# One product for the edge rows of both batches, first weights split ahead of the roots, and a wait for stored keys moved, in the values of a second cross-attention

## The chip, the cores and the metric

The kernel runs on one core of a Trainium2 chip. The metric is the device time of one execution in microseconds. The median of three executions is 3082.03 us (3081.09, 3082.03 and 3088.36).

Engines are named as the profile names them: PE (TensorE, matmuls), PEld (its weight loads), DVE (VectorE), ACT (ScalarE), POOL (GpSimd) and SP (SyncE, here only a queue of transfers).

## The reference, cut to what matters

The program is a decoder of two layers on x of 2 batches x 512 rows x 512 features, each layer with self-attention, cross-attention and a mixture of experts. The change lies in the cross-attention of the second layer. Its context is 2 batches x 1024 positions x 512 features. Positions 0 to 256 (257 of them) are image context with weights of their own, the others text context.

```python
def _L1_xattn_ref(x, context, q_w, q_b, k_w, k_b, v_w, v_b, ki_w, ki_b, vi_w, vi_b, o_w, o_b, nq_s, nkt_s, nki_s):
    B, S, _ = x.shape                       # 2, 512; H = 16 heads of D = 128, INNER = 2048
    img_ctx = context[:, :N_IMG]            # N_IMG = 257
    txt_ctx = context[:, N_IMG:]
    q = rms_norm(x @ q_w + q_b, nq_s).reshape(B, S, H, D)
    k_txt = rms_norm(txt_ctx @ k_w + k_b, nkt_s).reshape(B, -1, H, D)
    v_txt = (txt_ctx @ v_w + v_b).reshape(B, -1, H, D)
    out_txt = sdpa(q, k_txt, v_txt)
    k_img = rms_norm(img_ctx @ ki_w + ki_b, nki_s).reshape(B, -1, H, D)
    v_img = (img_ctx @ vi_w + vi_b).reshape(B, -1, H, D)
    out_img = sdpa(q, k_img, v_img)
    out = (out_txt + out_img).reshape(B, S, INNER)
    return out @ o_w + o_b
```

## The kernel before, in words

The code writes one instruction stream per engine by hand, in blocks, with semaphores between them. A `Stage` owns buffers and semaphores. When it closes, its semaphores are cleared and all engines meet in a barrier, so a stage ends with its slowest engine, SP's queue included. Nothing is planned by a program; the order within an engine is the order of the code, and loops (`Fori`) repeat a body.

`cross_attention1` runs four stages. `project_kq1` makes keys and queries head by head (16 heads) and stores them to DRAM, and `project_v1` makes the values. `attention_core1` reads both back, and `output_cross1` projects. All fp32 operands are held as a high part (rounded to fp32r) and a low part (the rest), and `split_matmul` (lines 2032 to 2034) makes one product of three matmuls: high x high, high x low, low x high. The context lies transposed in `ctx_high` and `ctx_low`, as 128 partitions x 4 slices of features (KC) x 2048 positions, batch 0 first.

**`project_v1`.** Its output has 2048 columns, in NG = 4 groups of 512. In a group there are UT = 16 tiles of 128 context rows (2 batches x 8). A tile's product is 4 slices x 3 matmuls = 12 matmuls. The stationary operand is 128 context positions, the moving one 512 columns of weights. `UNITS` orders the tiles, numbered from 0: four image tiles (NI = 4), then the two *edge tiles* (tiles 4 and 5, position block 2 of each batch), then ten text tiles. An edge tile holds positions 256 to 383: position 256 is image, the others text. So an edge tile is computed with the text weights, and once more with the image weights into another bank (4 + b), of which only row 0 is used:

```python
for kind, bank in [(m, t % 4)] + ([(0, 4 + b)] if kb == EDGE else []):   # line 2376
```

TensorE uses banks t % 4 and waits until the row addition four tiles back is done (`rowed`). DVE adds the bias (line 2448; for an edge tile also row 0 from the other bank, line 2452), ACT rounds to the high part (line 2411), POOL subtracts for the low part (line 2475), and SP stores both parts (line 2343), with four buffers in turn, so that ACT waits for a store four tiles back.

At the head of the stage TensorE sums the squares of the keys and queries with a matrix of ones (four matmuls of 512 columns, line 2384, and eight of one column, line 2387; each appears as two in the trace). ACT takes the roots (lines 2415 and 2419), then rounds the first image and text weights (line 2398, `split_weights`), and DVE subtracts for their low parts (line 2432). The first image weights were loaded during the keys' stage (`load_image`, line 1943). DVE takes four reciprocals of the roots (line 2456) between the tiles of the first group.

**The seam.** `project_kq1` ends, on SP, with a wait until all stored keys and queries have landed (line 2132). Its POOL adds squares up to the end (line 2282). Before the last group of `project_v1`, SP issues the core stage's first loads of keys and queries (`load_kq`, lines 1932 and 1933).

## Time and profile before

| What | Value |
|---|---|
| Timed runs: median (lowest, highest) | 3082.03 us (3081.09, 3088.36) |
| The profiled execution: its own time | 3078.52 us |
| Its span in the trace | 3076.7 us |
| Mean granted clock over it | 0.943 of full |
| TensorE busy | 2767.7 us (90%) |
| Weight loads busy | 1978.0 us (64%) |
| VectorE, ScalarE, GpSimd busy | 1461.4, 1288.5, 1108.3 us |
| Stage of the values | about 1613.8 to 1832 us |

All stretches are in microseconds from the start of the span. A matmul's busy time counts from its start to its modelled end, so matmuls overlap, and the distance from start to start is what one costs in a row of them. Weight loads run beside matmuls. The granted clock is 1.00 at 2.4 GHz and 0.50 at 1.2 GHz. An idle time is put down to the instruction that ended it. Names are the program's, without numbers: `xa` is the cross-attention, `early` the buffer of the image weights, `wt` that of the text weights, `normed` the buffer in which the rows wait, `ps` the banks.

### The profile page before, as it was taken

The page shows a single profiled execution, that of the slowest core. Times are in us where ns is not written, and L with a number is a line of the kernel's source. Part 1 is how long each engine was busy: PE and PEld are TensorE (multiplying, and loading weights), DVE is VectorE, ACT ScalarE, POOL GpSimd, SP SyncE. Part 2 cuts the span into 40 slices and gives each one's busy share as a digit, 9 for nine tenths or more (in the row PEclk, how much of TensorE's full clock was granted, in tenths as well). Part 3 has the DMA queues.
Part 4 walks back from the last instruction along what each step waited for, and adds up shares of the span by engine and source line. Part 5 has one row for each costly group of instructions (what it writes and reads, how often), then busy time and mean ns, then how long its engine had stood idle before and what let it go on. Part 6 is the DMA issues. An engine that isn't in the chain of part 4 may idle for free. (4 is left out here: it accounts for less than half of the span.)

```text
span 3076.7 us, 47541 instructions
## 1 busy us (share of the span) xinstructions
PE 2767.7 (90%) x15658; PEld 1978.0 (64%) x15658; DVE 1461.4 (47%) x2628; ACT 1288.5 (42%) x2906; POOL 1108.3 (36%) x1023
## 2 busy tenths in 40 slices
PE   7987999996699598879999989999998879999997
PEld 3453443432588345568877879999997647777762
DVE  3475436775211307678874337776663441111115
ACT  2462524554111126556652228888882202222220
POOL 2352225664111205435553445555551011212116
PEclk9899999997699798999999999999999889999998
DMA  2342424310599413156666773444431119999986
GB/s 92 70 96 82 161 87 102 64 32 4 183 326 317 155 41 83 43 181 237 236 235 192 222 233 139 184 186 174 170 150 59 50 54 339 345 346 346 345 272 210
DMA packets 320543, 526.50 MB, mean 171 GB/s; under 512 B 35778, under 2 KB 169282, under 8 KB 312228
## 3 DMA queue, kind: packets, MB, share of 16 engines
q1 hardware_dynamic: 292004, 453.61, 45.2%
q0 software_dynamic: 13440, 44.05, 4.7%
q10 hardware_dynamic: 14976, 27.27, 2.4%
q8 instruction: 69, 1.13, 0.2%
q14 instruction: 54, 0.44, 0.0%
HBM read 369.52 MB, written 130.02 MB: 162 GB/s over the span
## 5 line engine op out<-in xcount | busy, mean ns | idle before, releaser
L1741 PE MATMUL ps<-moe_blocks_xgt,moe_blocks_w 128*128 128x128 f32 (+1 forms) x3072 | 362.8, 277 | 7.1 <-DMA moe_blocks_b1s<-rb_cols 4.3
L1741 PEld LDWEIGHTS ps<-moe_blocks_xgt,moe_blocks_w 128*128 128x128 f32 (+1 forms) x3072 | 350.4, 184 | 10.3 <-issue 10.1
L2670 POOL TENSOR_TENSOR normed<-normed,xa_core_rinv 128x257 f32<-128x257 f32 (+1 forms) x256 | 260.6, 1041 | 214.0 <-DVE xa_core_rinv L2594 214.0
L1812 DVE COPY moe_blocks_y<-ps 128x512 f32<-128x512 f32 x104 | 72.0, 692 | 454.3 <-PE ps L1723 454.3
L1723 PE MATMUL ps<-moe_blocks_w,moe_blocks_ht 128*128 128x512 f32 (+1 forms) x624 | 285.0, 593 | 0.0
L550 POOL TENSOR_TENSOR sa_w<-sa_w,sa_core_rinv 128x256 f32<-128x256 f32 (+3 forms) x128 | 159.4, 1254 | 236.5 <-DVE sa_core_rinv L497 236.5
L1689 POOL COPY moe_blocks_idx<-moe_index 128x1 uint32 (+1 forms) x104 | 19.2, 185 | 561.8 <-PE ps L1714 435.2
L2650 ACT ACTIVATE normed<-normed,xa_core_nmax,xa_rq 128x257 f32<-128x257 f32 (+1 forms) x256 | 206.8, 810 | 4.2
L2282 POOL TENSOR_TENSOR normed<-normed 128x512 f32<-128x512 f32 x96 | 150.5, 1568 | 116.9 <-DVE normed L2235 116.9
L1762 ACT ACTIVATE moe_blocks_xgt<-ps 128x512 f32<-128x512 f32 x104 | 62.1, 597 | 304.1 <-PE ps L1714 304.1
L787 DVE TENSOR_REDUCE xa_nmax<-ps 128x1 f32<-128x1024 f32 x128 | 149.2, 1217 | 58.6 <-PE ps L778 58.6
L1723 PEld LDWEIGHTS ps<-moe_blocks_w,moe_blocks_ht 128*128 128x128 f32 (+1 forms) x624 | 111.0, 191 | 100.4 <-issue 100.4
L2609 DVE CUSTOM_DVE_ANT_0 normed<-ps,xa_rk 128x257 f32<-128x257 f32 (+1 forms) x256 | 164.6, 681 | 15.2 <-PE ps L2034 10.6
L527 ACT ACTIVATE sa_w<-ps,sa_core_nmax 128x128 f32<-128x128 f32 (+3 forms) x256 | 132.4, 524 | 83.5 <-DVE sa_core_nmax L493 82.3
L2600 DVE TENSOR_TENSOR xa_core_pt<-ps,xa_core_pt 128x512 fp32r<-128x512 f32 x256 | 164.6, 684 | 3.6 <-ACT xa_core_pt L2640 3.5
L2640 ACT ACTIVATE xa_core_pt<-ps 128x512 fp32r<-128x512 f32 x256 | 139.1, 596 | 64.2 <-PE ps L2572 63.8
L2032 PE MATMUL ps<-xa_core_pt,xa_core_v 128*128 128x256 f32 x512 | 155.2, 303 | 0.1
L452 PE MATMUL ps<-identity,sa_w 128*128 128x128 f32 x640 | 122.9, 302 | 30.8 <-DVE normed L506 17.1
L2034 PE MATMUL ps<-xa_core_pt,xa_core_v 128*128 128x256 f32 x512 | 144.9, 283 | 0.0
L2033 PE MATMUL ps<-xa_core_pt,xa_core_v 128*128 128x256 f32 x512 | 144.6, 282 | 0.0
L1791 ACT ACTIVATE moe_blocks_ht<-ps,moe_blocks_b1s 128x128 f32<-128x128 f32 (+1 forms) x240 | 69.9, 362 | 178.1 <-PE ps L1741 178.1
L2475 POOL TENSOR_TENSOR xa_v_parts<-normed,xa_v_parts 128x512 fp32r<-128x512 f32 x64 | 89.6, 1401 | 127.2 <-ACT xa_v_parts L2411 127.2
(333 smaller groups left out, 6525.3 us busy)
## 6 DMA issues: line engine op xcount, KB each, us to landing
moe_blocks_w<-L_ffn_rw SPq DMA_DIRECT2D x80, 704.0 KB
moe_blocks_w<-L_ffn_rw SPq DMA_DIRECT2D x80, 512.0 KB
moe_blocks_w<-L_ffn_w SPq DMA_DIRECT2D x24, 1408.0 KB
k_parts<-xa_parts SPq DMA_DIRECT2D x64, 512.0 KB, 3.3
v_parts<-xa_v_parts SPq DMA_DIRECT2D x128, 256.0 KB, 2.7
xa_parts<-k_parts SPq DMA_DIRECT2D x32, 1024.0 KB
xa_core_v<-v_parts SPq DMA_DIRECT2D x32, 1024.0 KB
moe_y<-moe_blocks_y ACTq DMA_DIRECT2D x104, 256.0 KB
```

What stands on the lines that cost most here:

```text
L550: nc.gpsimd.tensor_tensor(prob[:, 2 * s:2 * s + 2, 0:n], prob[:, 2 * s:2 * s + 2, 0:n], rinv[:, s, :, 0:1].to_broadcast([P, 2, n]), ALU.mu ...
L787: nc.vector.tensor_reduce(self.nmax[:, i % 2, m:m + 1], g.ps[:, bank:bank + 2, :].rearrange("p a n -> p (a n)"), X_AXIS, ALU.max, negate=T ...
L1723: mm = nc.tensor.matmul(g.ps[:, 6 + s % 2, :], ht[0:fn, s % 2, f, :], w2s[s][0:fn, f, :], start=(f == 0), stop=(f == NF - 1))
L1741: mm = nc.tensor.matmul(g.ps[0:fn, 2 + s % 2 + 2 * half, f * P:(f + 1) * P], w1s[s][:, k, half * F + f0:half * F + f0 + fn], xgt[:, s % 2, ...
L2032: nc.tensor.matmul(out, lhs_high, rhs_high, start=start, stop=False)
L2033: nc.tensor.matmul(out, lhs_high, rhs_low, start=False, stop=False)
L2034: return nc.tensor.matmul(out, lhs_low, rhs_high, start=False, stop=stop)
L2282: nc.gpsimd.tensor_tensor(sums[:, u * 512:(u + 1) * 512], sums[:, u * 512:(u + 1) * 512], sq[:, u % 2, :], ALU.add).then_inc(summed, 1)
L2600: nc.vector.tensor_tensor(pt[:, slot, 1, 4 * half:4 * half + 4, at:at + P], g.ps[:, 4 + half, :].rearrange("p (m q) -> p m q", m=4), pt[:, ...
L2609: ins = nc.vector.tensor_tensor_reduce(prob[:, n % PR, lo:hi], s_ps(n)[:, lo:hi], rk[:, b * CTX + lo:b * CTX + hi], 1.0, -3.4e38, ALU.mult ...
L2650: ins = nc.scalar.activation(prob[:, n % PR, lo:hi], prob[:, n % PR, lo:hi], ACT.Exp, scale=rq[:, t:t + 1], bias=nmax[:, n % PR, m:m + 1], ...
L2670: ins = nc.gpsimd.tensor_tensor(prob[:, n % PR, lo:hi], prob[:, n % PR, lo:hi], rinv[:, n % PR, m:m + 1].to_broadcast([P, hi - lo]), ALU.mult)
```

## The change

Three things change.

First, the image product of the edge rows. In a group it is computed once, in bank 4, ahead of the first edge tile (t == NI). The stationary operand is taken from the flat context with a step: 128 columns, 16 elements apart, beginning at position 256 of batch 0. Column 0 is that position, and column 64 the one 1024 further, position 256 of batch 1. The other 126 columns are not used. For the last feature slice the stepped columns run past the end of the context, so both context buffers get 256 more columns, which POOL fills with zeros in the keys' stage. DVE reads row 64 instead of row 0 for batch 1.

Second, ACT rounds the first image weights ahead of the roots, and the first text weights behind them as before.

Third, SP's wait for stored keys and queries moves from the end of the keys' stage to the place in `project_v1` right ahead of `load_kq`. The six semaphores now belong to the stage around both.

```diff
--- before.py
+++ after.py
@@ -29,6 +29,7 @@
 DX = 128
 INNER = H * DX
 NIMG = 257
+EDGE_PAD = NIMG // P * P
 LN_EPS = 1e-5
 RMS_EPS = 1e-6
 TOPK_EPS = 1e-20
@@ -1933,8 +1934,8 @@
             sp.dma_start(q[:, s, :, :].bitcast(F32), q_dram[j, :, :, :]).then_inc(kq_loaded[s], 16)
 
         with Stage(nc, name + "_made") as md:
-            ctx_high = md.sbuf("ctx_high", [P, KC, B * CTX], F32R)
-            ctx_low = md.sbuf("ctx_low", [P, KC, B * CTX], F32R)
+            ctx_parts = [md.sbuf(f"ctx_{part}", [P, KC * B * CTX + EDGE_PAD], F32R) for part in ("high", "low")]
+            ctx_high, ctx_low = [t[:, 0:KC * B * CTX].rearrange("p (k n) -> p k n", k=KC) for t in ctx_parts]
             early = md.sbuf("early", [P, KC * 512])
             wi = early[:, :].rearrange("p (k n) -> p k n", k=KC)
             wi_loaded = md.sem("wi_loaded")
@@ -1943,10 +1944,13 @@
                 sp.dma_start(wi, a["L1_xattn_vi_w"][:, bass.ds(n * 512, 512)].rearrange("(k p) n -> p k n", p=P)
                              ).then_inc(wi_loaded, 16)
 
+            stored = [md.sem(f"stored{u}") for u in range(6)]
             with Stage(nc, name + "_kq") as kq:
-                project_kq1(nc, g, kq, a, ctx_high, ctx_low, k_dram, q_dram, rk, parts, early, load_image)
+                project_kq1(nc, g, kq, a, ctx_high, ctx_low, k_dram, q_dram, rk, parts, early, load_image, stored,
+                            [t[:, KC * B * CTX:].bitcast(F32) for t in ctx_parts])
             with Stage(nc, name + "_v") as vs:
-                project_v1(nc, g, vs, a, ctx_high, ctx_low, v_dram, rk, rq, minus_rq, wi, wi_loaded, load_image, load_kq)
+                project_v1(nc, g, vs, a, ctx_high, ctx_low, v_dram, rk, rq, minus_rq, wi, wi_loaded, load_image, load_kq,
+                           stored, ctx_parts)
         ot = st.sbuf("ot", [P, B * H, S])
         with Stage(nc, name + "_core") as co:
             attention_core1(nc, g, co, k, q, kq_loaded, load_kq, v_dram, rk, rq, minus_rq, ot)
...
@@ -2064,7 +2068,6 @@
     x_highs, x_lows = st.sem("x_highs"), st.sem("x_lows")
     b_loaded, made, done, lows = st.sem("b_loaded"), st.sem("made"), st.sem("done"), st.sem("lows")
     squared, summed, zeroed = st.sem("squared"), st.sem("summed"), st.sem("zeroed")
-    stored = [st.sem(f"stored{n}") for n in range(UH)]
     scaled = st.sem("scaled")
 
     def load_weights(sp, h):
@@ -2128,8 +2131,6 @@
             sp.wait_ge(w_lows, H)
             load_image(sp, 0)
             store(H - 1)
-            for u in range(UH):
-                sp.wait_ge(stored[u], 16 * H)
 
         @block.tensor
         def _(pe):
@@ -2285,6 +2286,8 @@
             pool.wait_ge(x_lows, 1)
             nc.gpsimd.memset(sums[:, :], 0.0).then_inc(zeroed, 1)
             pool.wait_ge(zeroed, 1)
+            for pad in pads:
+                nc.gpsimd.memset(pad, 0.0).then_inc(zeroed, 1)
             head(0, 0, first=True)
             head(0, 1, first=True)
             with pool.Fori(1, H // 2) as i:
@@ -2292,7 +2295,8 @@
                 head(i, 1)
 
 
-def project_v1(nc, g, st, a, ctx_high, ctx_low, v_dram, rk, rq, minus_rq, wi, wi_loaded, load_image, load_kq):
+def project_v1(nc, g, st, a, ctx_high, ctx_low, v_dram, rk, rq, minus_rq, wi, wi_loaded, load_image, load_kq,
+               kq_stored, ctx_parts):
 
 
     NKT = CTX // P
@@ -2353,6 +2357,8 @@
             load_bias(0, 1)
             with sp.Fori(0, NG - 1) as n:
                 group(n)
+            for done in kq_stored:
+                sp.wait_ge(done, 16 * H)
             for s in range(2):
                 load_kq(sp, s, s)
             group(NG - 1, last=True)
@@ -2363,6 +2369,10 @@
         def _(pe):
             def tile(ctx, m, b, kb, k):
                 return ctx[:, k, b * CTX + kb * P:b * CTX + (kb + 1) * P]
+
+            def edges(ctx, k):
+                first, apart = k * B * CTX + EDGE * P, B * CTX // P
+                return ctx[:, first:first + apart * P:apart]
 
             def group(n, first=False):
                 pe.wait_ge(w_lows, 2 * n + 1)
@@ -2373,11 +2383,13 @@
                         pe.wait_ge(rooted, t + 1)
                     else:
                         pe.wait_ge(rowed, UT * n + t - 3)
-                    for kind, bank in [(m, t % 4)] + ([(0, 4 + b)] if kb == EDGE else []):
+                    if t == NI:
                         for k in range(KC):
-                            mm = split_matmul(nc, g.ps[:, bank, :], tile(ctx_high, m, b, kb, k), tile(ctx_low, m, b, kb, k),
-                                              w_high[:, kind, k, :], w_low[:, kind, k, :], start=(k == 0),
-                                              stop=(k == KC - 1))
+                            split_matmul(nc, g.ps[:, 4, :], edges(ctx_parts[0], k), edges(ctx_parts[1], k), w_high[:, 0, k, :],
+                                         w_low[:, 0, k, :], start=(k == 0), stop=(k == KC - 1))
+                    for k in range(KC):
+                        mm = split_matmul(nc, g.ps[:, t % 4, :], tile(ctx_high, m, b, kb, k), tile(ctx_low, m, b, kb, k),
+                                          w_high[:, m, k, :], w_low[:, m, k, :], start=(k == 0), stop=(k == KC - 1))
                     mm.then_inc(made, 1)
 
             for c in range(B * CTX // 512):
@@ -2410,6 +2422,7 @@
                         act.wait_ge(stored[t % RING], (UT // RING * n + t // RING) * 32)
                     nc.scalar.activation(parts[:, t % RING, 0, :], rows[:, t % 2, :], ACT.Copy).then_inc(highs, 1)
 
+            split_weights(0, 0)
             for c in range(B * CTX // 512):
                 act.wait_ge(total, c + 1)
                 nc.scalar.activation(rk[:, c * 512:(c + 1) * 512], g.ps[:, c, :], ACT.Sqrt, scale=1.0 / INNER,
@@ -2418,7 +2431,6 @@
             act.wait_ge(eps_put, 1)
             nc.scalar.activation(rms_q[:, :], g.ps[:, 6, 0:NT], ACT.Sqrt, scale=float(DX) / INNER,
                                  bias=eps_q[:, 0:1]).then_inc(rooted, 1)
-            split_weights(0, 0)
             split_weights(0, 1)
             group(0, first=True)
             with act.Fori(1, NG - 1) as n:
@@ -2447,9 +2459,11 @@
                         dve.wait_ge(lows, UT * n + t - 1)
                     ins = nc.vector.tensor_tensor(rows[:, t % 2, :], g.ps[:, t % 4, :], bias[:, m, :], ALU.add)
                     if kb == EDGE:
+                        at = b * (P // B)
                         ins.then_inc(edged, 1)
                         dve.wait_ge(edged, B * n + b + 1)
-                        ins = nc.vector.tensor_tensor(rows[0:1, t % 2, :], g.ps[0:1, 4 + b, :], bias[0:1, 0, :], ALU.add)
+                        ins = nc.vector.tensor_tensor(rows[0:1, t % 2, :], g.ps[at:at + 1, 4, :], bias[at:at + 1, 0, :],
+                                                      ALU.add)
                     ins.then_inc(rowed, 1)
                     if first and t in (2, 4, 6, 8):
                         c = t // 2 - 1
```

ACT, from the end of the keys' stage into the first group of the values (`xa_rk` and `xa_v_rms_q` are the roots, `xa_v_w_high` the rounded weights), before:

```order
L2199 ACTIVATE xa_parts<-ps,xa_kq_bias 128x512
L2091 UNCONDITIONAL_BRANCH
L2394 UNCONDITIONAL_BRANCH
L2415 ACTIVATE xa_rk<-ps,rms_eps 128x512 x4
L2419 ACTIVATE xa_v_rms_q<-ps,xa_v_eps_q 128x8
L2398 ACTIVATE xa_v_w_high<-xa_made_early 128x2048
L2398 ACTIVATE xa_v_w_high<-xa_v_wt 128x2048
L2411 ACTIVATE xa_v_parts<-normed 128x512 x6
L2398 ACTIVATE xa_v_w_high<-xa_made_early 128x2048
```

and now:

```order
L2200 ACTIVATE xa_parts<-ps,xa_kq_bias 128x512
L2094 UNCONDITIONAL_BRANCH
L2406 UNCONDITIONAL_BRANCH
L2410 ACTIVATE xa_v_w_high<-xa_made_early 128x2048
L2428 ACTIVATE xa_rk<-ps,rms_eps 128x512 x4
L2432 ACTIVATE xa_v_rms_q<-ps,xa_v_eps_q 128x8
L2410 ACTIVATE xa_v_w_high<-xa_v_wt 128x2048
L2423 ACTIVATE xa_v_parts<-normed 128x512 x6
L2410 ACTIVATE xa_v_w_high<-xa_made_early 128x2048
```

The rounding of the image weights (from `xa_made_early`) has moved ahead of the five roots; the rounding of the text weights (from `xa_v_wt`) stays behind them.

SP at the seam, with what each row waits for. A semaphore is printed by the name of an earlier holder of its number, so only the count of names tells something here: the six at the branch that leaves the keys' stage are the six of the stored keys and queries. Before:

```order
L2106 DMA k_parts<-xa_parts 256x1x512 [waits sa0_proj_r_loaded] x4
L2106 DMA q_parts<-xa_parts 128x1024 [waits sa0_proj_r_loaded] x2
L2091 UNCONDITIONAL_BRANCH [waits xa0_proj_inverted,xa0_proj_shifted,xa0_proj_scaled,xa0_proj_clipped,xa0_proj_tops,xa0_proj_ctx_loaded1]
L2324 UNCONDITIONAL_BRANCH [waits barrier_Pool_Activation_PE_DVE_SP_release]
L2327 DMA xa_v_wt<-L_xattn_v_w 128x4x512
L2331 DMA xa_v_bias<-L_xattn_vi_b 128x512
```

and now, at the same place:

```order
L2109 DMA k_parts<-xa_parts 256x1x512 [waits xa0_proj_scaled] x4
L2109 DMA q_parts<-xa_parts 128x1024 [waits xa0_proj_scaled] x2
L2094 UNCONDITIONAL_BRANCH
L2328 UNCONDITIONAL_BRANCH [waits barrier_Pool_Activation_PE_DVE_SP_release]
L2331 DMA xa_v_wt<-L_xattn_v_w 128x4x512
L2335 DMA xa_v_bias<-L_xattn_vi_b 128x512
```

SP now ahead of the last group of the values:

```order
L2335 DMA xa_v_bias<-L_xattn_v_b 128x512
L2358 REGISTER_ALU
L2358 COMPARE_AND_BRANCH
L1933 DMA xa_parts<-k_parts 128x2048 [waits init_x_loaded2,init_x_loaded3,init_x_loaded1,init_loaded,init_x_loaded0,init_rstd_done]
L1934 DMA xa_parts<-q_parts 128x1024
```

The six waits have left the branch and stand at the first load of keys (line 1933 of the new file). On TensorE the program has 24 rows fewer, 12 in the group written out and 12 in the loop's body, and no row in another order. POOL has two memsets more, of 256 columns each, behind the one that clears the sums in the keys' stage.

## Rows read from the trace of the kernel before

**Rows 1.** The page: busy us, share of the span, instructions.

```profile
PE 2767.7 (90%) x15658; PEld 1978.0 (64%) x15658; DVE 1461.4 (47%) x2628; ACT 1288.5 (42%) x2906; POOL 1108.3 (36%) x1023
```

**Rows 2.** Groups, 1607.2 to 1832 us: busy, mean ns, idle before.

```profile
L2032 PE MATMUL ps<-xa_v_w_high,xa_made_ctx_high 128*128 128x512 f32 x288 | 113.4, 394 | 4.5 <-DVE xa_v_w_low L2432 4.5
...
L2475 POOL TENSOR_TENSOR xa_v_parts<-normed,xa_v_parts 128x512 fp32r<-128x512 f32 x64 | 89.6, 1401 | 127.2 <-ACT xa_v_parts L2411 127.2
...
L2448 DVE TENSOR_TENSOR normed<-ps,xa_v_bias 128x512 f32<-128x512 f32 x64 | 43.9, 689 | 121.0 <-POOL xa_v_parts L2475 61.1 <-PE ps L2034 56.2 <-issue 3.7
...
L2411 ACT ACTIVATE xa_v_parts<-normed 128x512 fp32r<-128x512 f32 x64 | 40.3, 631 | 150.1 <-DVE normed L2448 109.9 <-DVE normed L2452 33.6 <-DMA v_parts<-xa_v_parts 6.6
...
L2456 DVE RECIPROCAL xa_rk<-xa_rk 128x512 f32<-128x512 f32 x4 | 13.4, 3342 | 0.0
...
L2432 DVE TENSOR_TENSOR xa_v_w_low<-xa_v_wt,xa_v_w_high 128x2048 fp32r<-128x2048 f32 x4 | 9.1, 2282 | 0.0
...
L2452 DVE TENSOR_TENSOR normed<-ps,xa_v_bias 1x512 f32<-1x512 f32 x8 | 5.4, 679 | 0.3
```

**Rows 3.** Busy by stretches: us, each engine (instructions), clock, DMA, GB/s.

```profile
1618.30:1619.60 1.30, 1.30 (x5) 0.58 (x4) 0.00 (x0) 0.68 (x1) 0.00 (x0) 0.97 1.06 310
...
1619.60:1621.40 1.80, 1.80 (x17) 1.73 (x15) 0.00 (x0) 0.69 (x2) 0.00 (x0) 1.00 0.08 22
...
1621.80:1625.90 4.10, 0.00 (x1) 0.00 (x1) 2.35 (x2) 3.52 (x2) 0.00 (x0) 0.50 0.00 0
...
1625.90:1631.60 5.70, 5.70 (x13) 4.46 (x14) 2.53 (x4) 0.00 (x0) 0.00 (x0) 0.50 0.77 271
...
1674.00:1825.00 151.00, 150.91 (x666) 124.62 (x664) 48.76 (x61) 39.79 (x54) 71.59 (x50) 1.00 0.76 231
```

**Rows 4.** Waits, 1613.7 to 1832 us: us in total, times, longest.

```profile
ACT xa_v_parts L2411 <- DMA v_parts<-xa_v_parts: 6.6, 1, 6.6
...
PE ps L2032 <- DVE xa_v_w_low L2432: 4.5, 1, 4.5
```

**Rows 5.** Two in order of time, then the instructions of line 2132.

```profile
1607.09 3.06 SPq L2106 DMA_DIRECT2D q_parts<-xa_parts  x2
...
1609.25 1.64 POOL L2282 TENSOR_TENSOR normed<-normed 128x512 f32<-128x512 f32 x1 [1.07 <-DVE normed L2235]
...
L2132 SPq EVENT_SEMAPHORE  x3: 17/28/28, 1610.2 to 1612.4; - x3
```

**Rows 6.** Instructions in order of time: start us, us, engine, line.

```profile
1615.88 0.69 ACT L2415 ACTIVATE xa_rk<-ps,rms_eps 128x512 f32<-128x512 f32 x1 [7.43 <-PE ps L2384]
...
1619.57 1.84 PE L2387 MATMUL ps<-all_ones,normed 128*128 128x1 f32 x16
...
1621.62 1.90 ACT L2398 ACTIVATE xa_v_w_high<-xa_made_early 128x2048 fp32r<-128x2048 f32 x1
...
1623.55 2.29 DVE L2432 TENSOR_TENSOR xa_v_w_low<-xa_made_early,xa_v_w_high 128x2048 fp32r<-128x2048 f32 x1 [9.66 <-ACT xa_v_w_high L2398]
...
1625.90 0.79 PE L2032 MATMUL ps<-xa_v_w_high,xa_made_ctx_high 128*128 128x512 f32 x1 [4.48 <-DVE xa_v_w_low L2432]
```

**Rows 7.** Weight loads of 32 columns, grouped by shape.

```profile
L605 PEld LDWEIGHTS ps<-normed,xa_v 128*32 128x32 f32 x344 | 6.9, 109 | 14.8 <-issue 8.7 <-ACT normed L653 3.1 <-ACT xa_core_probs L653 3.0
```

**Rows 8.** In order of time, the next stage: one load, two matmuls.

```profile
2101.24 0.19 PEld L2033 LDWEIGHTS ps<-xa_core_pt,xa_core_v 128*128 128x128 f32 x1
...
2101.36 0.28 PE L2033 MATMUL ps<-xa_core_pt,xa_core_v 128*128 128x256 f32 x1
...
2102.56 0.28 PE L2034 MATMUL ps<-xa_core_pt,xa_core_v 128*128 128x256 f32 x1
```

**Rows 9.** In order of time, GpSimd at the start of the keys' stage.

```profile
1340.82 2.67 POOL L2286 MEMSET normed<- 128x3072 f32 x1 [56.58 <-DVE xa_kq_x_low L2257]
1348.88 1.40 POOL L2282 TENSOR_TENSOR normed<-normed 128x512 f32<-128x512 f32 x1 [5.40 <-DVE normed L2235]
```

**Rows 10.** Busy in a stretch of the last group, columns as in rows 3.

```profile
1788.00:1792.00 4.00, 4.00 (x19) 3.30 (x18) 0.00 (x0) 0.23 (x1) 1.29 (x1) 1.00 1.01 408
```

More of the change, by code:

```diff
@@ L2034, in split_matmul, with project_kq1 @@
     return nc.tensor.matmul(out, lhs_low, rhs_high, start=False, stop=stop)
-def project_kq1(nc, g, st, a, ctx_high, ctx_low, k_dram, q_dram, rk, parts_out, early, load_image):
+def project_kq1(nc, g, st, a, ctx_high, ctx_low, k_dram, q_dram, rk, parts_out, early, load_image, stored, pads):
     UH, RR = 6, 4
```

## The prediction

> **What bounds the kernel now.** The page comes first. TensorE is busy for 90% of the span [rows 1]. Then comes the stage of the change, the values of the second cross-attention (1613.8 to 1832 us), by its groups of instructions: 288 matmuls on each of three lines, 864, and beside them VectorE, ScalarE and GpSimd at 0.69, 0.63 and 1.40 us per tile of rows [rows 2]. Next the spacing of the matmuls, from the busy time by stretches: 666 in 151.0 us at full clock, 0.2267 us each, so a tile of 12 takes 2.72 us [rows 3]. The slowest follower (1.40 us) is far below 2.72, and in the list of waits TensorE has a single wait in the whole loop, 4.5 us on the first low weights at the start [rows 4]. So TensorE sets this stage, and a matmul that goes away is time that goes away. What is left is the seam in front of the stage: when the keys' stage lets go [rows 5], what runs until the first product [rows 6], and the clock granted there [rows 3].
>
> **The change part by part.** Sums are made against the profiled execution, 3078.52 us with a span of 3076.7.
>
> *Edge rows.* Each of the four column groups ran 12 matmuls for batch 0's edge row and 12 for batch 1's. Now 12 serve both. 4 x 12 = 48 matmuls go, 48 x 0.2267 = 10.9 us. VectorE's two one-row additions of 0.68 us per group stay [rows 2]; they only read partition 64 instead of 0 for the second batch. The two edge products now both run in front of the first edge tile, so tile 4 still takes 5.44 us and tile 5 only 2.72.
>
> What is new is how the stationary operand is read: 128 columns that lie 16 elements, 64 bytes, apart. No row of this trace has such a load, so I bound it. The nearest rows are the packed loads: 0.19 us for 128 columns [rows 8] and 109 ns for 32 [rows 7], so a column adds some (190 - 109) / 96 = 0.84 ns. How fast loads can follow one another shows in the next stage: 256-column matmuls come every 0.12 us (2101.36 to 2102.56, ten steps), each with its own 128-column load [rows 8]. So a load holds its path for at most 0.12 us, against the 0.227 that a 512-column matmul leaves. If a strided load took no longer, the cost is zero (below zero is excluded: a load off the bound can give nothing). If it took twice as long, 0.24 us, 48 x (0.24 - 0.227) = 0.6 us. If every column cost four packed ones, 0.48 us, it would be 48 x 0.25 = 12 us. I take zero, as the packed rows are nearest and even a doubling hides, and I keep 12 us for the range.
>
> The Trainium skill speaks against this read. "Advanced Engine Details and Errata", section "SBUF Cachelines", says that SBUF has lines of 16 bytes, that two hits on a line are needed to absorb the memory's latency, and that a different line for each access costs a penalty; 64 bytes is a new line for every column. It names no factor. A penalty of two would leave my sum where it is, one of four would take away the edge term; no row here shows either.
>
> *The wait for stored keys.* At the end of the keys' stage SP waits until its last stores have landed, until 1612.4; GpSimd's last addition ends at 1609.25 + 1.64 = 1610.9, SP's last issue at 1610.15 [rows 5]. With the wait gone the seam opens on GpSimd: 1612.4 - 1610.9 = 1.5 us earlier. The bounds are 0 (the barrier might cost more when GpSimd is last) and 1.5. The wait now stands ahead of the last group's loads of keys and queries, behind three groups of 16 tiles, well over 100 us later, when the stores are long down. Behind it in SP's queue are those loads and the last group's stores; as it never holds, they lose nothing.
>
> *First weights.* Before, ScalarE takes the five roots first, then from 1621.62 rounds the image weights (1.90 us), VectorE makes their low part (2.29 us), and TensorE, done with its one-column products at 1619.57 + 1.84 = 1621.41, stands until 1625.90 [rows 6]. Now the rounding is first: 1613.8 + 1.90 + 2.29 = 1618.0 on the old time line, 3.4 us before TensorE asks. ScalarE is free again at 1615.7, just ahead of its first root at 1615.88. So TensorE starts at 1621.41: 4.5 us. The text weights are split last (1621.6 + 1.90 + 2.28 = 1625.8, after which VectorE takes its first row) and are needed 4 x 2.72 = 10.9 us after the start, at 1632.3. The first row, ready at 1624.1, then waits some 2 us, which four banks absorb.
>
> *The clock.* It has risen to full by 1618.3, falls at 1621.8 when TensorE stands, and the first 1631.6 - 1625.9 = 5.7 us of products run at the lower level, 1.2 GHz [rows 3]. The 13 matmuls in it would take 13 x 0.2267 = 3.0 us at full clock. With no pause the products follow straight on the one-column ones. If the clock stays up, 2.7 us more. The bounds are 0 and 2.7; in this stage the trace keeps full clock wherever TensorE went on working, so I take 2.7.
>
> *The pads.* Two GpSimd memsets of 256 columns. One of 3072 columns took 2.67 us, so by columns 0.2 us each; a floor could make it a few tenths. They fall into the 5.4 us in which GpSimd stands before its first addition [rows 9]. Zero; without that cover under 1 us.
>
> *Does VectorE hold the first group?* It carries four reciprocals of 3.34 us and a split of 2.28 there [rows 2], and the two edge tiles now give it 2.72 us less. I stepped it through from TensorE's start: tile 7's row is ready at 29.4 us, and TensorE wants its bank (tile 11) at 32.6. The smallest slack is 3.2 us, so no stall.
>
> **Sum**: 10.9 + 1.5 + 4.5 + 2.7 = 19.6 us. 3078.5 - 19.6 = 3058.9 for a profiled execution. The median of the timed runs, 3082.03, lies 3.5 us above the profiled one, and against it the forecast is 3082.0 - 19.6 = 3062.4 us.
>
> **Rivals.**
> 1. *The clock drops once* in or behind the one-column products, which held full clock before but move few columns (1.8 us of them, [rows 3]). Then 2.7 comes back: 3065.1. For it: the clock fell within 0.4 us of their end. Against: the fall came with TensorE standing.
> 2. *Strided loads are dear but bearable*, four packed ones per column: 3062.4 + 12 = 3074.4, a gain of 7.6.
> 3. *Slower*: one mechanism, the strided load. The other terms are worth 8.7 us, the edge term 10.9. The kernel is slower than before once each of the 48 loads holds TensorE 19.6 / 48 = 0.41 us beyond 0.227, that is a load every 0.64 us, 5.3 times the 0.12 of [rows 8]. At 0.83 us each (seven times) the cost is 48 x 0.60 = 29 us, and the time 3091. For it: no such load was ever seen here. Against: it needs more than four lost accesses per column.
> 4. *The stores take over.* In the last group the queues are full (408 GB/s from 1788 to 1792, with the next stage's keys) and ScalarE waits 6.6 us for a landed store [rows 4, 10]. With tile 5 early by 2.7 us this wait could reach TensorE. For it: that wait exists. Against: beside it TensorE has no wait at all in the same list, and a row may be three tiles late (8 us) before TensorE notices. All groups hit would cost 4 x 2.7 = 10.9: 3073.3.
>
> **How the numbers follow.** Forecast (loads hidden, clock held) 0.52; rival 1 0.20; loads between two and four times as long, 3066 to 3072, 0.09; rival 2 0.08; rival 4 0.05; slower 0.06, of which 0.05 by over 0.3%. About 0.3%, 9.2 us, is what a measurement of this kernel can tell from no change, so faster means below 3072.8. Faster holds the forecast, rival 1 and the loads in between, and some of rival 4: 0.83. The rest near zero is rival 2, half of rival 4 and a slight loss: 0.12. Range: 3058 (the forecast less a scatter of some 4 us between medians) to 3074, next to rival 2; about one in seven is left above.
>
> **What would show it.** The matmuls of the stage must be 816. The SP wait of 2.1 us at the end of the keys' stage is gone, and TensorE starts its sums some 1.5 us nearer to the last addition. TensorE's wait of 4.5 us on the low weights is gone. The granted clock stays at 1.00 from the roots on. The 12 matmuls of an edge product lie 0.227 us apart like the others; a longer load shows in its own duration (about 0.30 us if doubled) before it shows in the spacing. I am wrong if the edge products are spaced wider than the rest, or if a new wait of TensorE on VectorE shows up in the first or last group.

## The result, and the profile after

The changed kernel takes 3065.56 us, the median of four runs (3058.73 to 3068.16); the kernel before took 3083.82 beside it (3081.09 to 3088.36). The ratio is 0.9936, with a 95% interval of 0.9915 to 0.9957, so 13 to 26 us less; the forecast was 19.6 less and 3062.4.

The page of the changed kernel, TensorE's and GpSimd's entries:

```profile
PE 2759.1 (90%) x15610; PEld 1973.0 (64%) x15610; DVE 1459.1 (48%) x2628; ACT 1288.6 (42%) x2906; POOL 1108.6 (36%) x1025
```

Against [rows 1] these are 48 matmuls and 8.6 us of TensorE less, and GpSimd's two memsets more. The groups of the stage, 1612.8 to 1818.7 us (busy us, mean ns, idle before):

```profile
L2036 PE MATMUL ps<-xa_v_w_high,xa_made_ctx_high 128*128 128x512 f32 x272 | 106.1, 390 | 0.0
...
L2423 ACT ACTIVATE xa_v_parts<-normed 128x512 fp32r<-128x512 f32 x64 | 40.3, 631 | 134.1 <-DVE normed L2460 102.3 <-DVE normed L2465 25.7 <-DMA v_parts<-xa_v_parts 6.1
...
L2465 DVE TENSOR_TENSOR normed<-ps,xa_v_bias 1x512 f32<-1x512 f32 x8 | 5.5, 682 | 0.3
```

Each of the three product lines has 272 matmuls instead of the 288 of [rows 2], and the 4.5 us that TensorE stood in front of them is 0.0. VectorE's one-row additions cost what they did, 682 ns. ScalarE still waits once for a landed store, 6.1 us ([rows 4]: 6.6), and as before nothing on TensorE comes of it.

The seam and the start of the stage in order of time (start us, us, engine, line):

```profile
1615.38 1.64 POOL L2283 TENSOR_TENSOR normed<-normed 128x512 f32<-128x512 f32 x1 [1.08 <-DVE normed L2236]
...
1617.86 1.91 ACT L2410 ACTIVATE xa_v_w_high<-xa_made_early 128x2048 fp32r<-128x2048 f32 x1 [3.29 <-PEq L68]
1617.88 5.77 PE L2396 MATMUL ps<-normed,all_ones 128*128 128x512 f32 x8 [4.61 <-PEq L68]
...
1619.80 2.29 DVE L2444 TENSOR_TENSOR xa_v_w_low<-xa_made_early,xa_v_w_high 128x2048 fp32r<-128x2048 f32 x1 [1.83 <-ACT xa_v_w_high L2410]
...
1623.48 1.84 PE L2399 MATMUL ps<-all_ones,normed 128*128 128x1 f32 x16
...
1625.19 0.48 PE L2036 MATMUL ps<-xa_v_w_high,xa_made_ctx_high 128*128 128x512 f32 x1
```

GpSimd's last addition ends at 1615.38 + 1.64 = 1617.02 and the sums start 0.86 us later; before it was 1613.80 - 1610.89 = 2.91 [rows 5]. The low weights are there at 1622.1, and the first product follows the one-column products without a gap. The same stretch by windows (us, each engine, granted clock, DMA share, GB/s), with the first edge product and a long stretch of plain tiles behind it:

```profile
1617.88:1622.00 4.12, 4.12 (x5) 1.82 (x6) 2.26 (x2) 2.90 (x3) 0.00 (x0) 0.50 0.78 248
1622.00:1623.50 1.50, 1.50 (x5) 0.58 (x4) 0.10 (x1) 1.03 (x2) 0.00 (x0) 0.97 0.94 359
1623.50:1625.20 1.70, 1.70 (x18) 1.70 (x16) 0.00 (x0) 0.70 (x2) 0.00 (x0) 1.00 0.65 178
1625.20:1631.00 5.80, 5.80 (x28) 4.78 (x28) 3.23 (x5) 2.35 (x3) 0.00 (x0) 1.00 0.39 144
1636.00:1638.56 2.56, 2.56 (x12) 2.56 (x11) 2.17 (x2) 0.35 (x1) 0.41 (x1) 1.00 0.99 291
1680.00:1805.00 125.00, 125.00 (x552) 104.84 (x551) 42.46 (x53) 34.19 (x47) 60.90 (x44) 1.00 0.81 250
```

The clock rises during the sums and stays: the products start at 1.00, where [rows 3] has 0.50 for 5.7 us. Plain tiles still come at 125.0 / 552 = 0.2265 us per matmul. In the edge product the weight loads, which were 0.19 us, fill the whole stretch (2.56 of 2.56). The last packed load, a strided one, and two of the product's matmuls, ten steps apart:

```profile
1635.75 0.19 PEld L2038 LDWEIGHTS ps<-xa_v_w_high,xa_made_ctx_low 128*128 128x128 f32 x1
...
1636.21 0.30 PEld L2037 LDWEIGHTS ps<-xa_v_w_low,xa_made_ctx_high 128*128 128x128 f32 x1
...
1636.21 0.40 PE L2036 MATMUL ps<-xa_v_w_high,xa_made_ctx_high 128*128 128x512 f32 x1
...
1638.56 0.40 PE L2037 MATMUL ps<-xa_v_w_low,xa_made_ctx_high 128*128 128x512 f32 x1
```

The load takes 0.30 us, and the matmuls come every (1638.56 - 1636.21) / 10 = 0.235 us.

For all kernels but one (the steps, whose values are not those of the others) I read the same marks from the order of time: last matmul of the keys' stage (the last needed one, where unneeded ones follow it), first sum, first product, first matmul of the core stage. Us between them:

| kernel | seam | sums to product | product to core | stage in all |
|---|---|---|---|---|
| before | 7.04 | 12.10 | 206.65 | 225.79 |
| before, again | 7.04 | 12.25 | 205.11 | 224.40 |
| changed | 5.00 | 7.31 | 193.47 | 205.78 |
| edges apart | 5.00 | 8.05 | 203.76 | 216.81 |
| roots first | 5.01 | 11.53 | 196.24 | 212.78 |
| roots first, kept busy | 5.00 | 12.60 | 193.50 | 211.10 |
| wait back | 7.01 | 8.22 | 193.48 | 208.71 |
| 65 columns | 5.00 | 6.66 | 196.61 | 208.27 |
| kept warm | 5.03 | 5.21 | 196.64 | 206.88 |
| 65 columns, full pad | 5.00 | 7.32 | 193.37 | 205.69 |
| kept warm, full pad | 5.03 | 5.21 | 193.41 | 203.65 |
| pad 8 more | 5.00 | 7.48 | 198.40 | 210.88 |
| pad 16 more | 5.00 | 7.51 | 198.28 | 210.79 |

The stage is 225.79 - 205.78 = 20.0 us shorter.

### The profile page after: what moved, and what is told of

Its sections match the earlier page's. It is cut to its first block and busy times, and to the rows that moved or that the text cites. A ratio compares the mean times of both kernels' runs of the same rounds, so it can differ in the third digit from the quotient of the medians.

```text
span 3066.4 us, 47445 instructions
## 1 busy us (share of the span) xinstructions
PE 2759.1 (90%) x15610; PEld 1973.0 (64%) x15610; DVE 1459.1 (48%) x2628; ACT 1288.6 (42%) x2906; POOL 1108.6 (36%) x1025
## 5 line engine op out<-in xcount | busy, mean ns | idle before, releaser
L2623 DVE CUSTOM_DVE_ANT_0 normed<-ps,xa_rk 128x257 f32<-128x257 f32 (+1 forms) x256 | 164.6, 681 | 15.4 <-PE ps L2038 10.9
L2036 PE MATMUL ps<-xa_made_ctx_high,xa_kq_w_high 128*128 128x256 f32 (+2 forms) x384 | 124.7, 325 | 12.4 <-DVE xa_made_ctx_low L2254 9.1
```

What stands on the lines that cost most here:

```text
L2036: nc.tensor.matmul(out, lhs_high, rhs_high, start=start, stop=False)
L2623: ins = nc.vector.tensor_tensor_reduce(prob[:, n % PR, lo:hi], s_ps(n)[:, lo:hi], rk[:, b * CTX + lo:b * CTX + hi], 1.0, -3.4e38, ALU.mult ...
```

## The experiments

### The kernel before, once more

No edit; it shows what one trace differs from the next by.

> The kernel before once more, for its trace. It tells what part of the two traces' difference outside the stage is scatter: in the changed kernel's trace the keys' stage and what lies before it came 6.1 us later, and the rest after it 3.6 us. Theory (scatter of landing transfers): these parts move by several us from trace to trace of one kernel, while the stage (225.8 us) stays within 0.5. Rival (the wider context buffers or the pads cost something there): they stay at the values of the first trace.

3078.95 us. What follows the stage is 1247.3 us instead of 1244.2. The stage is 1.4 us shorter than in the first trace, where at most 0.5 was expected. The pause is the same, 4.5 us, but behind it the lower clock lasted 2.8 us (seven matmuls) and not 5.7, so the first products cost 1.5 us less. A difference of this size between two single traces shows nothing about an edit, unless the rows say where it lies.

### Edges apart

```
-  if t == NI: ... split_matmul(g.ps[:, 4, :], edges(...), ...)
+  for kind, bank in [(m, t % 4)] + ([(0, 4 + b)] if kb == EDGE else []):
...
-  g.ps[at:at + 1, 4, :], bias[at:at + 1, 0, :]
+  g.ps[0:1, 4 + b, :], bias[0:1, 0, :]
```

> Computes all of the reference. Undone alone: the shared edge product; each edge tile has its image product again, with packed loads, in its own bank. Theory (the term of 10.9 us): the stage, measured from the last matmul start of the keys' stage to the first matmul start of the core stage (205.8 us in the changed kernel), grows by 48 x 0.2267 = 10.9 less the 48 x 0.009 = 0.4 that the strided loads cost, to 216.3 us. Time about 10 us over the changed kernel. Rival (the stores or VectorE had taken over): the stage grows by less than 8 us and TensorE shows a wait on VectorE in the changed kernel's loop.

3073.38 us (11 runs, 3070.20 to 3079.53), ratio 0.9970 [0.9958, 0.9982]; stage 216.81 against the 216.3 expected, with 0.7 us of it in the sums. The first of its product lines:

```profile
L2036 PE MATMUL ps<-xa_v_w_high,xa_made_ctx_high 128*128 128x512 f32 x288 | 112.1, 389 | 0.0
```

From product to core the changed kernel is 203.76 - 193.47 = 10.3 us shorter, and by the ratios (0.9970 - 0.9936) x 3082 = 10.5. This is the edge term.

### Roots first, and roots first with TensorE kept busy

`split_weights(0, 0)` stands behind the roots again. The second kernel also gives TensorE 18 unneeded 512-column matmuls between the one-column products and the first product. Both compute all of the reference.

```
-  split_weights(0, 0)
   for c in range(B * CTX // 512): ... ACT.Sqrt ...
+  split_weights(0, 0)
   split_weights(0, 1)
...
+  for d in range(18):   # the second kernel alone, TensorE
+      nc.tensor.matmul(g.ps[:, 5, :], ctx_high[:, 0, 0:P], ctx_high[:, 0, 0:512], ...)
   group(0, first=True)
```

> Computes all of the reference. Undone alone: the order on ScalarE; the five roots come before the first image weights again. Theory: TensorE stands 4.5 us again after its one-column products and starts at the lower clock, 2.7 us more, so the stage is 205.8 + 7.2 = 213.0 us. Rival (the clock was no matter of the pause, but of where the stage lay): 4.5 us only, 210.3, at full clock.

> As e2_roots_first, but TensorE runs 18 matmuls of 512 columns into a bank nobody reads while it would stand. Computes all of the reference. Theory (the pause lets the clock fall, and the fall costs 2.7 us by itself): the clock stays at 1.00, the stage is 213.0 - 2.7 = 210.3 us. Rival (the clock depends on what went before, not on the pause): the clock falls as in e2_roots_first and the stage stays at 213.

Roots first: 3070.02 us (4 runs, 3067.85 to 3073.43), ratio 0.9960 [0.9945, 0.9975], an interval that overlaps the changed kernel's; its stage of 212.78 us is the 213.0 expected. Kept busy, one run: 3066.07, stage 211.10 against 210.3 (its sums took 6.43 us). Two windows and the wait of TensorE for the first kernel, then the same for the second:

```profile
1622.00:1626.40 4.40, 0.03 (x1) 0.00 (x0) 2.23 (x2) 3.86 (x3) 0.00 (x0) 0.91 0.00 0
...
1626.50:1632.20 5.70, 5.68 (x13) 4.46 (x14) 2.53 (x4) 0.00 (x0) 0.00 (x0) 0.50 0.74 271
```

```profile
PE ps L2036 <- DVE xa_v_w_low L2444: 4.5, 1, 4.5
```

```profile
1622.00:1626.40 4.40, 4.28 (x19) 3.19 (x18) 2.21 (x2) 3.88 (x3) 0.00 (x0) 1.00 0.00 0
...
1626.50:1632.20 5.70, 5.66 (x25) 4.69 (x26) 3.16 (x4) 0.63 (x1) 1.08 (x1) 1.00 0.79 253
```

```profile
PE ps L2036 <- DVE xa_v_w_low L2446: 0.3, 1, 0.3
```

With the pause back, the clock is at 0.50 for the first products: 13 matmuls in 5.7 us, the very row of before. With the pause filled by work that nobody needs, the weights come just as late, but the clock stays at 1.00 and 25 matmuls fit. From product to core that is 196.24 against 193.50, 2.7 us. So the order of ScalarE's work is worth two separate things: the 4.5 us of standing still in the wait's row (4.2 by the marks, since the eight sums took 5.37 us in that trace and 5.77 in the changed kernel's), and 2.7 us of clock that the standing cost. No other event is needed for the drop. The second price is that of these traces: with the edges apart, where the same 864 matmuls as before start at full clock, product to core is 203.76 us, so the low clock cost 206.65 - 203.76 = 2.9 us in the first trace of before and 205.11 - 203.76 = 1.4 in the second.

### Wait back

```
   store(H - 1)
+  for u in range(UH): sp.wait_ge(stored[u], 16 * H)      # end of the keys' stage
...
-  for done in kq_stored: sp.wait_ge(done, 16 * H)        # ahead of the last loads
```

> Computes all of the reference. Undone alone: SP waits for the stored keys and queries at the end of the keys' stage again. Theory: from the last matmul of the keys' stage to the first sum 7.0 us instead of 5.0, the rest of the stage as in the changed kernel: 207.8 us. Rival (the seam opens on GpSimd or the barrier anyway, and the 2.0 us came from elsewhere): 5.0 us stay. The forecast had named 1.5.

3065.44 us (4 runs, 3063.33 to 3072.74), ratio 0.9945 [0.9930, 0.9960]. The last addition on GpSimd and the first sum:

```profile
1619.99 1.64 POOL L2285 TENSOR_TENSOR normed<-normed 128x512 f32<-128x512 f32 x1 [1.07 <-DVE normed L2238]
...
1624.50 2.90 PE L2396 MATMUL ps<-normed,all_ones 128*128 128x512 f32 x3 [6.62 <-PEq L68]
```

From 1621.63 to 1624.50 are 2.87 us where the changed kernel has 0.86, so the wait costs 2.0, not the 1.5 forecast. The timed runs agree in size, (0.9945 - 0.9936) x 3082 = 2.8 us, but their intervals overlap, so it is the seam in the trace that shows it. The stage is 2.9 us longer, 208.71 against the 207.8 expected; the other 0.9 lies in the eight sums, 6.69 us instead of 5.77.

### Steps of the stationary operand

Each 128-column weight load reads its columns 1, 4, 8 or 16 elements apart in the values' stage, and 1, 2, 4 or 8 apart in the core's value products (lines 2042 to 2044 step 1, 2048 step 2, 2054 step 4, 2060 step 8, 2066 step 16). They are the wrong columns, so this kernel leaves out the values of this cross-attention.

```
-  split_matmul(..., tile(ctx_high, m, b, kb, k), tile(ctx_low, m, b, kb, k), ...)
+  step = (1, 4, 8, 16)[k]
+  SPLIT[step](..., stepped(ctx_parts[0], step, k), stepped(ctx_parts[1], step, k), ...)
```

> Leaves the right operands out: in the values' stage and in the core stage's product with the values the stationary operand is read with a step, from the wrong places, so the values of this cross-attention are not computed. Steps are 1, 4, 8, 16 elements (4 to 64 bytes) beside 512-column matmuls, and 1, 2, 4, 8 beside 256-column matmuls, each step on a line of its own. Theory (a stepped column costs two packed ones once it leaves the 16-byte line of its neighbour): 0.30 us per load for steps of 4 and up, 0.19 below; spacing 0.235 beside 512 columns, and beside 256 columns 0.12 for steps 1 and 2 but 0.22 to 0.24 for steps 4 and 8. Rival (the cost grows with the step): 16 is dearer than 4. Rival (only the latency of a load grows): 0.12 us spacing stays for all steps beside 256 columns.

3159.2 us, one run. Weight loads by line (busy us, mean ns), first beside 512-column products, then in the core stage beside 256 columns:

```profile
L2042 PEld LDWEIGHTS ps<-xa_v_w_high,xa_made_ctx_high 128*128 128x128 f32 x64 | 12.0, 188 | 0.0
...
L2054 PEld LDWEIGHTS ps<-xa_v_w_high,xa_made_ctx_high 128*128 128x128 f32 x64 | 19.7, 308 | 3.0
...
L2060 PEld LDWEIGHTS ps<-xa_v_w_high,xa_made_ctx_high 128*128 128x128 f32 x64 | 20.5, 320 | 0.0
L2066 PEld LDWEIGHTS ps<-xa_v_w_high,xa_made_ctx_high 128*128 128x128 f32 x64 | 20.3, 317 | 0.0
...
L2048 PEld LDWEIGHTS ps<-xa_core_pt,xa_core_v 128*128 128x128 f32 x128 | 25.3, 197 | 0.0
```

```profile
1951.99 0.28 PE L2049 MATMUL ps<-xa_core_pt,xa_core_v 128*128 128x256 f32 x1
1952.11 0.28 PE L2050 MATMUL ps<-xa_core_pt,xa_core_v 128*128 128x256 f32 x1
...
1952.23 0.39 PE L2054 MATMUL ps<-xa_core_pt,xa_core_v 128*128 128x256 f32 x1
1952.46 0.40 PE L2055 MATMUL ps<-xa_core_pt,xa_core_v 128*128 128x256 f32 x1
```

Steps of 4 and 8 bytes load in 188 to 197 ns and let 256-column matmuls come every 0.12 us. From 16 bytes on a load takes 0.30 to 0.34 us, and with steps of 16 and 32 bytes they come every 0.23 to 0.25. A step of 64 bytes was tried beside 512 columns alone; its load, 0.30 to 0.32 us, is no dearer than that of 16. So a strided load holds up the next one about twice as long as a packed one, and beside 512 columns, which take 0.227 us anyway, nearly all of that is covered: in the edge product the spacing is 0.235. "Advanced Engine Details and Errata", section "SBUF Cachelines" of the Trainium skill, puts the line at 16 bytes with two hits wanted on each; free steps up to 8 bytes and dear ones from 16 agree with it, and the factor of two is from these runs.

### 65 columns, and kept warm

The edge product needs only columns 0 and 64, so 65 stepped columns will do and the pad need not be zeroed; the pad was cut to 8 elements as well. The second kernel adds unneeded matmuls: 16 at the end of the keys' stage and 22 at the end of the values' stage, behind its last product.

```
-  return ctx[:, first:first + apart * P:apart]
+  return ctx[:, first:first + apart * (P // B) + 1:apart]
...
-  for pad in pads: nc.gpsimd.memset(pad, 0.0).then_inc(zeroed, 1)
...
-  EDGE_PAD = NIMG // P * P
+  EDGE_PAD = 8
```

> Computes all of the reference. The edge product takes only 65 stepped columns (0 and 64 are the ones used), so no pads and no memsets. Theory (loads cost by column): a load of 65 columns takes about 0.19 us even at the doubled price, the edge matmuls are 0.227 us apart, the stage is 205.8 - 0.4 = 205.4 us. Rival (a stepped load costs a fixed amount more): 0.235 us apart as before. Without pads it also shows the keys' stage with buffers of nearly the old size: if its length is as in the kernel before, 283.7 us from the first layer-norm row to the last matmul start, every time, the pads cost 4 us there; if it scatters, they don't.

> Computes all of the reference. As e7_65_columns, and TensorE runs matmuls that nobody reads where it would stand: 16 at the end of the keys' stage, 22 at the end of the values' stage. Theory (the clock falls only while TensorE stands, and 1.3 us at a barrier are too short): the sums run at full clock, 2.2 us less up to the first product (then bound by the low weights), and the core stage's first matmuls too, 2.6 us less: 200.6 us for the stage and some 5 us in all. Rival (the clock falls at the barrier anyway, or the extra matmuls hold up the stage's end): no gain, or a loss.

3069.72 us (one run) and 3070.15 (8 runs, 3064.76 to 3079.08; ratio 0.9960 [0.9945, 0.9974]). Both miss: stages of 208.3 and 206.9 us, where 205.4 and 200.6 were expected. In the second the clock stayed up through the first seam, but at the start of the core stage it fell after four matmuls all the same (from there they came every 0.43 us). The load of 65 strided columns does take 0.19 us, as expected. What is new is the spacing of every plain product, 125.0 us with 543 matmuls instead of 552 (the first of the two kernels):

```profile
1680.00:1805.00 125.00, 125.00 (x543) 101.55 (x542) 41.77 (x52) 33.61 (x46) 60.25 (x43) 1.00 0.83 246
```

Over all 816 matmuls it is 0.2314 us against 0.2275, so 3.2 us. Two things could have done it: the output of 65 rows, or the shorter pad, which moves every buffer behind it.

### The same with the full pad, and a longer pad alone

```
-  EDGE_PAD = 8
+  EDGE_PAD = NIMG // P * P         # 65 columns and kept warm
...
-  EDGE_PAD = NIMG // P * P         # the changed kernel, nothing else
+  EDGE_PAD = NIMG // P * P + 8     # or + 16
```

> 65 stepped columns and no zeroing of the pad, as in the run with 65 columns, but with the pad left at 256 elements, so that every buffer has the address that it has in the changed kernel (the run with 65 columns had a pad of 8 elements). That run's matmuls of the values' stage came every 0.2310 us instead of 0.2267 (816 of them, 3.4 us). If the moved addresses did it, the spacing is 0.2267 to 0.2275 here and the stage, from the last matmul of the keys' stage to the first of the core, is 205.0 to 205.6 us (the changed kernel's 205.8, less 0.65 us for the wait on the zeroed pad, which would be late by then). If the output of 65 rows did it, it is 0.231 again and 208.3 us.

> The changed kernel with a pad of 264 elements instead of 256: nothing is computed differently, the second buffer of the values' operand begins 32 bytes later and what is allocated behind both 64 bytes later. If addresses set the spacing, the matmuls of the values' stage come every 0.231 us instead of 0.2275 and the stage takes 209 us; if the size of the offset matters only with 65 rows, 0.2275 and 205.8 us.

> The changed kernel with a pad of 272 elements: the second buffer of the values' operand begins 64 bytes later than in the changed kernel and what is allocated behind both 128 bytes later. With 264 elements (32 and 64 bytes later) the matmuls of the values' stage came every 0.2336 us instead of 0.2275, and the stage took 210.9 us instead of 205.8. If what costs is a buffer that begins off a multiple of 64 bytes, the spacing is 0.2275 again and the stage 205.8 us. If any offset from the old places costs, or one off a multiple of 128 bytes or more, it is 0.231 to 0.234 and 208.5 to 211 us.

> As the run that is kept warm (65 columns, 16 unneeded matmuls ahead of the seam and 22 behind it), with the pad left at 256 elements. That run's stage took 206.9 us at a spacing of 0.2310. If the addresses cost it that: 816 x 0.0043 = 3.5 us less, 203.4 us, and the kernel 2.4 us faster than the changed one on the median, if the rest stays. If the 65 rows did it: 206.9 us again, and the same median as the changed kernel within 2 us.

One run each for the first three: 3064.26, 3074.61, 3070.16 us. Their plain products in this order:

```profile
1680.00:1805.00 125.00, 125.00 (x552) 103.34 (x551) 42.44 (x53) 33.85 (x47) 61.26 (x43) 1.00 0.82 249
```

```profile
1680.00:1805.00 125.00, 125.00 (x537) 102.34 (x536) 41.66 (x52) 32.97 (x45) 59.79 (x42) 1.00 0.81 244
```

```profile
1680.00:1805.00 125.00, 125.00 (x538) 102.52 (x537) 41.79 (x52) 33.55 (x46) 58.97 (x43) 1.00 0.83 245
```

With the old addresses the 65 rows cost nothing, and they gain next to nothing: the stage is 205.69 us against the changed kernel's 205.78, its edge matmuls 0.233 us apart instead of 0.235. With the addresses moved by 32 and 64 bytes, or by 64 and 128, and not one instruction changed, each matmul of the stage takes 3% longer, the stage 5 us. The keys' stage reads the same buffers and is slower too; here 200 us of it in the changed kernel, then with 65 columns and the short pad:

```profile
1400.00:1600.00 200.00, 200.00 (x1154) 176.61 (x1153) 166.70 (x182) 124.04 (x242) 112.55 (x73) 1.00 0.67 237
```

```profile
1400.00:1600.00 200.00, 200.00 (x1148) 176.26 (x1147) 165.54 (x179) 122.71 (x238) 111.42 (x72) 1.00 0.67 235
```

From its 97th matmul to its last it takes 242.5 us in all nine traces of the table with the placement of before or of the changed kernel, and 244.3 to 244.4 in the four with another. So another placement costs 1.8 us there on top. The theory that a start off a multiple of 64 bytes is what costs has fallen with the last of the three. Nor is it the distance moved alone: the short pad lies 32 and 64 bytes off the places of before and runs at 0.231 us, the pad with 8 more lies as far off those of the changed kernel and runs at 0.233. Which of the buffers it is, and what distance is free, stays open: the two placements that ran at 0.2267 are the one of before and the one 1024 and 2048 bytes further.

Kept warm with the full pad: 3065.43 us (6 runs, 3062.22 to 3068.35), ratio 0.9947 [0.9935, 0.9959]. That is 4.7 us less than with the short pad, where the two stages in the traces give 3.2 + 1.8 = 5.0; the intervals of the two ratios overlap. Its sums and what follows:

```profile
1613.13 3.67 PE L2397 MATMUL ps<-normed,all_ones 128*128 128x512 f32 x8 [0.96 <-PEq L68]
1616.64 1.84 PE L2400 MATMUL ps<-all_ones,normed 128*128 128x1 f32 x16
```

The eight sums take 3.67 us instead of 5.77, and the stage 203.65, near the 203.4 expected and 2.1 less than in the changed kernel. Of the 4.8 us that the first expectation set on a held clock that is what came inside the stage; the other 2.6 were set on the core stage, where the clock fell again. The medians are 3065.43 and 3065.56, so the 2.4 us expected are not seen, and an interval of some 4 us to either side could not show them: no version here beats the changed kernel by what can be measured.

## Why the prediction was right

*TensorE sets the stage*: right. With 48 matmuls fewer the stage shrank by their time, and TensorE has no wait on VectorE in the changed kernel.

*Edge rows*, 10.9: measured 10.3, by the comparison with the edges apart. The working allowed a doubled load 0.6 us, and a doubled load it was: 0.30 us, spacing 0.235, so 48 x 0.008 = 0.4. The profile showed it in the duration first and hardly in the spacing, as was said. I took zero where a doubling was the truth; the sum hardly noticed, since 512 columns cover it. Beside 256 columns it would have: there steps of 16 and 32 bytes double the spacing. Rivals 2 and 3, with loads four and seven times as long, are out: at 64 bytes, too, the load takes 0.30 us.

*The wait for stored keys*, 1.5: measured 2.0. The mis-sized term: I took the time from the last arrival to the next stage's first matmul as the same whoever is last, 1.4 us behind SP [rows 5]. Behind GpSimd it is 0.86 us.

*First weights*, 4.5: from sums to product 12.10 - 7.31 = 4.8 in the first pair of traces, 4.2 in the pair that differs in this edit alone, and 4.5 in the wait's own row. Right.

*The clock*, 2.7: the mechanism is right, and the size here is 196.24 - 193.47 = 2.8 or, with the gap filled, 196.24 - 193.50 = 2.7. That it fits to 0.1 us is partly luck: by the second trace of before the same pause cost 1.4 us of clock, and the sum would have been 18.3. Rival 1 is out in all: the one-column products end at 1.00 and what follows stays there.

*The pads*, zero: right in size. The memsets take 0.32 us each, 0.6 together, and GpSimd stands for 6.07 us behind them. One of them, and the addition that ends the gap:

```profile
1346.74 0.32 POOL L2290 MEMSET xa_made_ctx_high<- 128x256 f32 x1
...
1353.38 1.47 POOL L2283 TENSOR_TENSOR normed<-normed 128x512 f32<-128x512 f32 x1 [6.07 <-DVE normed L2236]
```

What I had not asked is what the pad's length does to the addresses: 8 or 16 elements more would have taken 5 of the 20 us back, and 1.8 us in the keys' stage. With the 256 elements that the change takes, TensorE's spacing is that of before. That this length was free is luck; nothing in the prediction weighed it.

*The stores take over* (rival 4): did not happen; ScalarE's 6.1 us wait reached nobody.

The sum of the stage, 20.0 against 19.6, is closer than its parts deserve: 0.6 too much for the edges, against 0.5 too little at the seam and 0.3 at the weights. Against the second trace of before it is 18.6. The profiled execution itself is another matter: 3068.16 us against the 3058.9 that its own sum gave, though its stage is right. It lies 9.3 us above, since the trace has 6.1 us more ahead of the stage and 3.6 more behind it than that of before. Of the 6.1 us, 2.9 lie in the keys' stage, 276.6 us against 273.7 from its first product to its last. One stretch of its start, before and then changed:

```profile
1350.00:1370.00 20.00, 17.25 (x100) 14.88 (x99) 20.00 (x21) 12.12 (x23) 12.30 (x9) 1.00 0.67 235
```

```profile
1350.00:1370.00 20.00, 16.72 (x82) 14.39 (x83) 16.90 (x20) 12.88 (x29) 10.50 (x7) 0.91 0.43 159
```

The clock was at 0.91 there. The difference lies in the first 96 matmuls of that stage, 34.0 us against 31.2. The kernels with edges apart, roots first, kept busy and wait back run the same code there as the changed one, and took 31.4, 31.0, 31.6 and 33.6 us; with 65 columns and the full pad, where nothing is zeroed, it was 33.4. So the same code gives both lengths, and the zeroed pads do not make the long one. What does is open. The other 3.3 us lie ahead of that stage's first product, which starts at 1331.7 and 1333.1 us in the two traces of before and at 1334.0 to 1341.4 in the eleven others of the table. Two traces of before are too few to call this scatter or a price of the change; it stays open. The timed medians, 18.3 us apart, fit the stage within their interval, which would also hold a loss of a few us elsewhere.

## What to carry to other kernels

Where one engine sets a stage, price a cut by its spacing, not by the duration of its instructions, and ask of a new access pattern what covers it: a load twice as dear was nearly free beside 512 columns and doubled the spacing beside 256. The pause of 4.5 us was paid twice here, once in standing and once in the clock behind it (1.4 to 2.9 us by the trace), so work that ends such a pause should come ahead of work with later users. When a buffer's size changes, measure with the old placement too, before the difference is put down to the code.

## What the runs showed of the hardware

- A 128-column fp32 weight load takes 0.19 us with columns 4 or 8 bytes apart and 0.30 to 0.34 with 16, 32 or 64.
- The matmuls of plain tiles came every 0.2267, 0.2310 or 0.2333 us at the same granted clock, by where the buffers lay (for the first and the last nothing else was changed). In the keys' stage the dearer placements cost 1.8 us of 242.5. Neither DMA share (0.81 to 0.83) nor clock (1.00) differs between them.
- The seam between two stages costs 0.86 us behind GpSimd's last addition, and 2.87 behind it when SP still waits for stores.
- The eight sums behind the seam take 5.1 to 6.7 us when the clock starts at its lower level, and 3.67 with the clock held.
- Behind the same pause of 4.5 us the lower clock lasted 5.7 us in two traces and 2.8 in a third. With the pause filled by unneeded matmuls it did not fall.
